# Gated cross-attention block: the last batch by halves of its queries, the last row tile's GELU and product in pieces, and new orders of all five engines

## What is computed

```
x = x + tanh(gx) * attention(layernorm(x), ctx, mask)     # 8 heads of 64, softmax, W_o, b_o
h = gelu(bitlinear(layernorm(x), w1, b1))                 # 512 -> 2048
x = x + tanh(gf) * bitlinear(h, w2, b2)                   # 2048 -> 512
bitlinear(x, w, b): x / rms(x), rounded to 8 bit by its row's largest |x|;
                    w rounded to -1, 0, 1 by its mean |w|; product, + b
```

## Time and profile before

| | |
|---|---|
| median of 3 runs | 1093.64 us (1092.78 to 1095.91) |
| the profiled execution: its time, its span | 1094.15 us, 1092.3 us |
| PE busy | 1025.8 us (94% of the span) |
| ACT, DVE, POOL busy | 856.0, 793.5, 768.4 us |
| mean granted TensorE clock | 0.979 |

### The profile page before, as it was taken

How to read it: one execution, slowest core, us unless ns; L and a number is a source line. 1 busy time by engine, 2 the same in 40 slices (tenths; PEclk the granted TensorE clock), 3 DMA queues, 4 the chain that set the end, 5 groups by cost and what they waited for, 6 DMA issues and landing times.

```text
span 1092.3 us, 23652 instructions
## 1 busy us (share of the span) xinstructions
PE 1025.8 (94%) x8372; PEld 614.6 (56%) x8372; DVE 793.5 (73%) x1620; ACT 856.0 (78%) x1445; POOL 768.4 (70%) x739
## 2 busy tenths in 40 slices
...
GB/s 302 210 219 156 181 138 191 137 151 148 156 167 122 173 169 133 165 141 188 118 188 126 144 178 139 182 119 187 141 144 150 140 184 136 159 122 155 151 63 81
DMA packets 480004, 170.76 MB, mean 156 GB/s; under 512 B 458256, under 2 KB 460048, under 8 KB 479504
## 3 DMA queue, kind: packets, MB, share of 16 engines
...
## 4 chain that ended last, share of the span: by engine, by line
PE 72%; POOL 10%; DMA 8%; ACT 4%; DVE 3%; issue 3%; SPq 1%; ACTq 0%; POOLq 0%; DVEq 0%
PE ps_g L548 36%; PE ps_s L578 10%; PE ps_g L645 9%; PE ps_g L601 8%; PE ps_g L637 8%; POOL p L991 5%; DMA pt<-p 4%; PE ps_g L589 2%; DMA hqt<-hq 2%; DMA xqt<-xq 1%; POOL p L986 1%; POOL ctx L1002 1%; ACT hq L937 1%; SPq L510 1%; DMA pt<-in_ctx 1%
## 5 line engine op out<-in xcount | busy, mean ns | idle before, releaser
L991 POOL TENSOR_TENSOR p<-prob,p 112x750 f16<-112x750 f32 x256 | 404.0, 1594 | 107.7 <-ACT p L879 106.2
L706 DVE CUSTOM_DVE_ANT_0 prob<-ps_s,mbias 112x750 f32<-112x750 f32 x256 | 232.1, 933 | 114.8 <-PE ps_s L578 114.1
L872 ACT ACTIVATE prob<-prob,rmin 112x750 f32<-112x750 f32 x256 | 233.4, 913 | 30.9 <-DVE rmin L706 30.5
L548 PE MATMUL ps_g<-ctx,wk 128*128 128x375 f16 x1152 | 198.8, 325 | 17.3 <-DVE wk L663 15.9
L548 PE MATMUL ps_g<-wv,ctx 128*128 128x512 f16 (+1 forms) x864 | 195.3, 380 | 1.2 <-DVE k_sb L728 0.9
L548 PEld LDWEIGHTS ps_g<-ctx,wk 128*128 128x128 f16 x1152 | 109.1, 98 | 95.6 <-issue 28.6
L578 PE MATMUL ps_s<-k_sb,q_sb 64*112 64x375 f16 x1536 | 149.2, 327 | 5.3 <-DVE rmin L706 5.3
L548 PEld LDWEIGHTS ps_g<-wv,ctx 128*128 128x128 f16 (+1 forms) x864 | 88.5, 103 | 96.5 <-DVE q_sb L733 1.9
L879 ACT ACTIVATE p<-prob 112x750 f16<-112x750 f32 x160 | 127.6, 817 | 16.1 <-DMA pt<-p 15.9
L601 PE MATMUL ps_g<-pt,v_sb 128*64 128x224 f16 x2304 | 123.8, 262 | 4.3 <-DMA pt<-p 3.7
L578 PEld LDWEIGHTS ps_s<-k_sb,q_sb 64*112 64x112 f16 x1536 | 89.4, 126 | 55.0 <-issue 34.9
...
## 6 DMA issues: line engine op xcount, KB each, us to landing
...
pt<-p SPq DMA_TRANSPOSE x256, 4.1
...
```

What stands on the lines that cost most here:

```text
L548: mm = nc.tensor.matmul(out, lhs, rhs, start=(m == 0), stop=(m == len(steps) - 1))
L706: nc.vector.tensor_tensor_reduce(prob[:, (b * NU + n) % PROBS, :].rearrange("p (c k) -> p c k", c=2), ps_s[0:HT, n % 2, :, 0:CH], mbias[:, ...
L872: nc.scalar.activation(prob[:, (b * NU + n) % PROBS, :], prob[:, (b * NU + n) % PROBS, :], ACT.Exp, bias=rmin[:, n:n + 1], scale=-1.0, acc ...
L991: nc.gpsimd.tensor_tensor(p16[:, u % HILO, 1, 0:J], prob[:, (b * NU + n) % PROBS, :], p16[:, u % HILO, 0, 0:J], ALU.subtract).then_inc(s[" ...
```

## The change

Three things are changed.

1. **The last batch goes by halves of its queries.** In batch 15 unit m is half m // 4 of pair m % 4: first all four pairs for queries 0 to 111, then all four for queries 112 to 223. There are eight products PV:0..7:15 of 112 columns in place of four of 224, eight PA, PL and R. O:0:15 (tile 26) needs PL of the first half alone, O:1:15 (tile 27) that of both. T:u:15 waits for its own place in `pt` unit by unit.
2. **The last tile in pieces.** For tile 27 the GELU (ZE), the squares (ZS), the maximum (ZM) and the rounding (Z3) go by quarters of 512 columns, ZA joins the quarters' maxima and sums, and the transposing (ZT) and F2:1:15 go in two halves.
3. **All orders are new.** `cycle` runs for b = 1..13 and no longer to 14; `end` holds the rest of batch 14 and batch 15, whose steps are mixed.

```diff
-FIRST, LAST = 1, 15
+FIRST, LAST = 1, 14
...
+        def pair_and_half(b, m):
+            return (m % NP, m // NP) if b == LB else (m // 2, half_of(b, m))
+        def queries_of(b):
+            return HT if b == LB else TQ
+        def attn_pieces(b, n):
+            size = queries_of(b)
+            at = (b * TQ + (n // NP * HT if b == LB else 0)) % RINGQ
+            first = min(size, RINGQ - at)
+            return [(0, at, first)] + ([(first, 0, size - first)] if first < size else [])
...
-                    need(sp, "weighted", 0, (b * NM + n // 2 - TURNED) // 2)
+                    if b == LB and n // 2 >= TURNED:
+                        need(sp, "weighted", b, n // 2 - TURNED)
+                    else:
+                        need(sp, "weighted", 0, (b * NM + n // 2 - TURNED) // 2)
...
+                elif kind == "ZT":
+                    sp.wait_ge(z_hq, NF // 2 * (n + 1))
+                    part = slice(n * F // 2, (n + 1) * F // 2)
+                    sp.dma_start_transpose(tail_hqt[:, n * KF // 2:(n + 1) * KF // 2, :], tail_hq[:, part])\
+                        .then_inc(d_zt[n], 16)
...
-                            mm = nc.tensor.matmul(g[e * DH:(e + 1) * DH, 0:TQ]
-                                                  .rearrange("p (a q) -> p a q", a=2),
-                                                  v_sb[:, p, t, va, (2 * n + e) * DH:(2 * n + e + 1) * DH],
+                            mm = nc.tensor.matmul(g[e * DH:(e + 1) * DH, 0:queries_of(b)]
+                                                  .rearrange("p (a q) -> p a q", a=len(units)),
+                                                  v_sb[:, p, t, va, (2 * j + e) * DH:(2 * j + e + 1) * DH],
...
-                    need(pe, "attn_lo", b, 2 * NP - 1)
+                    need(pe, "attn_lo", b, 2 * (NM if t == NR - 1 else NP) - 1)
...
+                        if t == NR - 1 and k % (KF // 2) == 0:
+                            pe.wait_ge(d_zt[k // (KF // 2)], 16)
...
+                elif kind == "ZM":
+                    dve.wait_ge(z_gelu, n + 1)
+                    nc.vector.tensor_reduce(maxs_z[:, n:n + 1], tail_h[:, n * 512:(n + 1) * 512], AX.X, ALU.max,
+                                            apply_absolute_value=True).then_inc(z_max, 1)
...
+                elif kind == "ZE":
+                    part = slice(n * 512, (n + 1) * 512)
+                    need_tile(act, "h_lin", NR - 1, n)
+                    nc.scalar.activation(tail_h[:, part], tail_h[:, part], ACT.Gelu).then_inc(z_gelu, 1)
+                elif kind == "ZS":
+                    part = slice(n * 512, (n + 1) * 512)
+                    act.wait_ge(z_gelu, n + 1)
+                    nc.scalar.activation(tail_hq[:, part], tail_h[:, part], ACT.Square, accum_out=sums_z[:, n:n + 1])\
+                        .then_inc(z_sq, 1)
```

More of the change, by code:

```diff
@@ L15 @@
 NB = 16
+LB = NB - 1
 TQ = 224
@@ L331, in build @@
         hi_act, hi_pool = sem("hi_act"), sem("hi_pool")
+        z_gelu, z_sq, z_max, z_hq = sem("z_gelu"), sem("z_sq"), sem("z_max"), sem("z_hq")
+        d_zt = [sem(f"d_zt{n}") for n in range(2)]
         d_res = [sem(f"d_res{n}") for n in range(HELD)]
@@ L566, in emit @@
                 if kind == "S":
-                    j, half = n // 2, half_of(b, n)
-                    if n % 2 == 0:
+                    j, half = pair_and_half(b, n)
+                    if n < NP if b == LB else n % 2 == 0:
                         need(pe, "q_lo", b, j)
@@ L585, in emit @@
                     need(pe, "recips", b, n)
-                    for m in range(2 * n, 2 * n + 2):
-                        at = 256 + half_of(b, m) * HT
+                    units = [n] if b == LB else [2 * n, 2 * n + 1]
+                    j = n % NP
+                    for m in units:
+                        at = 256 + (0 if b == LB else half_of(b, m) * HT)
                         for e in range(2):
@@ L591, in emit @@
                                              ident[0:HT, 0:HT], start=True, stop=True)
-                    for u in range(b * NU + 4 * n + 4 - HILO, b * NU + 4 * n + 4):
+                    for u in range(b * NU + 2 * units[0], b * NU + 2 * units[-1] + 2):
                         need_turned(pe, u)
@@ L595, in emit @@
                         need(pe, "v_lo", b, NT - 1)
-                    places = sorted((place_of(b, 2 * n), place_of(b, 2 * n + 1)))
-                    both = slice(places[0], places[1] + 1, places[1] - places[0])
+                    places = sorted(place_of(b, m) for m in units)
+                    both = slice(places[0], places[-1] + 1, max(1, places[-1] - places[0]))
                     steps = [(t, va, pa) for t in range(NT) for va, pa in ((0, 0), (1, 0), (0, 1))]
@@ L805, in emit @@
                                                    op0=ALU.mult, op1=ALU.add).then_inc(s["h_lin"], 1)
+                elif kind == "ZM":
+                    dve.wait_ge(z_gelu, n + 1)
+                    nc.vector.tensor_reduce(maxs_z[:, n:n + 1], tail_h[:, n * 512:(n + 1) * 512], AX.X, ALU.max,
+                                            apply_absolute_value=True).then_inc(z_max, 1)
+                elif kind == "ZA":
+                    c = (NR - 1) % 2
+                    dve.wait_ge(z_max, NF)
+                    nc.vector.tensor_reduce(smh[:, c, 2:3], maxs_z[:, :], AX.X, ALU.max).then_inc(s["h_max"], 1)
+                    dve.wait_ge(z_sq, NF)
+                    nc.vector.tensor_reduce(smh[:, c, 7:8], sums_z[:, :], AX.X, ALU.add).then_inc(s["h_sq"], 1)
                 elif kind == "GM":
@@ L883, in emit @@
                     need(act, "attn_raw", b, n - 1)
-                    nc.scalar.activation(rb[:, :], g[:, 256:256 + TQ], ACT.Copy).then_inc(s["recips_out"], 1)
+                    nc.scalar.activation(rb[:, 0:queries_of(b)], g[:, 256:256 + queries_of(b)], ACT.Copy).then_inc(s["recips_out"], 1)
                 elif kind == "PL":
```

170 lines of the change are left out of this document (97 added, 73 removed).

## The result

| | before | after |
|---|---|---|
| median of 7 runs each, us | 1095.91 (1092.78 to 1099.55) | 1089.88 (1084.89 to 1092.93) |
| ratio | 1 | 0.9938, 95% interval 0.991 to 0.9966 |
| profiled execution, its span, us | 1094.15, 1092.3 | 1088.55, 1086.8 |

The kernel is faster by 0.62% (6.0 us between the medians), where 1.3% was forecast; 1089.88 lies just inside the range. Five marks in PE's timeline divide the span. The first line is us from the start of the span, the others are distances in us.

A forecast was written before the change was run, and what follows sets the result against it. PE was taken as the bound from 120 to about 1010 us, its waits and a serial chain at start and end. Terms -1.5 - 1.5 - 1.6 - 2.67 - 6.9 = -14.2 gave span 1078.1, median 1079.5 us; range 1070 to 1091.

The forecast's parts named there:

- the start: The new start lists on all engines, before the steady cycles: -1.5 us, bounds -6 and +4.
- the difference of 3.1 and 1, less a little: In the start: S:4:0 and V:0:1 moved earlier (1.1 and 2 us), against about 1 us net for L:2 and L:3 later.
- the 10.4 us: PE's wait for a bank in the start of the kernel before, which moved steps were to fill in part.
- The wait near 52 us under 8: Sign in the new profile: PE's long wait in the start falls below 8 us.
- The cycle: The steady orders, 13 cycles: PE's waits for `hqt` go, -1.5 us, bounds -5.4 and +6.5.
- no new kind over 3 us: Sign in the new profile: from 125 to 940 us no new kind of PE wait exceeds 3 us.
- The rival of a stall in each cycle: ACT's L4 waits for DVE's L3, delaying PE's F1: 2.2 us per cycle, 13 times, +28.6, 1108 us; chance 0.10.
- The end up to the last PV: The end through the last product PV: PV:7 ends at 1044.8 against 1046.43 before, -1.6 us.
- rival one: Narrow PV products cost as much as wide ones: +4 us, 1083.5, or +10.8, 1090.3, at serial loads; chance 0.13.
- rival two: The two halves don't get ahead, POOL's wait at L:7:15 passing delays through: 1083.5 to 1087.5 us; chance 0.17.
- The last projection: Behind the last PV, one tile's output projection of 2.67 us where two took 5.34: -2.67 us.
- The tail: From the end of the last projection to the span's end: 31.5 us where before it took 38.4, -6.9.

The follow-up runs named there:

- e3: The changed kernel with GELU, squares, maximum, rounding and turning of tile 27 undivided; 1092.74 us, ratio 0.9963 to the kernel before.
- e4: The changed kernel with ACT's three context splits ahead of the two of x in the start, as before; 1086.95 us, ratio 0.9906.
- e9: The kernel of e4 with the scores of unit 3 (S:3:0) put back ahead of Q:3:0 on PE; 1087.44 us, ratio 0.9913.
- e8: The kernel of e1, with POOL waiting ahead of the low part of unit 1 until DVE has centred batch 2's queries; 1080.95 us, ratio 0.9854.
- e11: The kernel of e4, with POOL waiting ahead of WB:6:0 until DVE has rounded piece 4 (WQ:4:0); 1081.57 us, ratio 0.9861.
- e12: The kernel of e4 with POOL's start list of before, the other four engines' lists new; 1089.83 us, ratio 0.9934.
- e10: The kernel of e4 with the sums for the first mean (WA:2 to WA:7) ahead of E:1:0, H:0:0 and H:1:0 on ACT; 1087.64 us, ratio 0.9909.
- e14: The kernel of e11 with matmuls that nothing reads filling four idle stretches of PE in the end; 1080.69 us, ratio 0.9859.
- e15: The kernel of e14, with POOL waiting ahead of WB:4:0 as well, until DVE has rounded piece 2; 1079.96 us, ratio 0.9852.
- e2: The kernel before with only the new cycle lists; 1091.34 us, ratio 0.9944.
- e1: The changed kernel with the five start lists of before, on all engines; 1081.19 us, ratio 0.9847 to the kernel before.

## Why the prediction was wrong

The direction held and the size did not: the step that failed is **the start**. It stood in the sum with -1.5, bounds -6 and +4, "the difference of 3.1 and 1, less a little". Measured is +4.1, and +7.9 and +8.2 in e3 and e4. Point by point:

- **The start, the overlap.** The 3.1 us were S:4:0 and V:0:1, which were to "fill a part of the 10.4 us". They could not: PE runs its list in order, the step that waits is Q:0:1, and in both lists both steps stand behind it. They could fill only the 0.90 us that PE waited for `pt` ahead of PV:0:0. The new list even moves S:3:0 (1.17 us) from ahead of the wait to behind it, and S:4:0 then waited 2.00 for `rmin`. What moving S:3:0 back is worth isn't shown (e9). "The wait near 52 us under 8" failed: 10.06.
- **The start, the hold-up.** I put DVE's share at nothing, and never asked why it came so late to empty V:4. The row that answers it lay in the trace before: two centrings in 4.95 us beside POOL's work. The new order puts a W2 rounding in that place. Taking the centring's hold-up away gains nothing (e8), since PE then waits for the turned queries and the turned parts. For the rounding ACT waits, with V:5:0 and the next roundings behind it. In the profiles of e4 and e11 taking a part of this hold-up away is worth 2.9 us directly; 4.2 more lie at the clock behind it, which e9 and e12 show can differ without it. By the medians, e4, e9 and e10 have ratios of 0.9906 to 0.9913 and e11, e14 and e15, with POOL's wait, 0.9852 to 0.9861: some 5 of the 10 us that the new start costs. The rest stays open; the late first product (2.1 us) may be a part (e4).
- **The cycle.** -1.5 forecast, -1.9 in the kernel after, -3.6 in e2 and -4.0 in e1. The waits for `hqt` went, and those for `pt` nearly. But "no new kind over 3 us" failed: the low part brings 4.4, so by its waits the kernel after gains next to nothing here, and that -1.9 is so near to the forecast is in part luck. The rival of a stall in each cycle asked for 1.35 us in each. A wait does recur in 12 cycles, which I had named as a sign of being wrong, but of 0.4 us at most.
- **The end up to the last PV.** -1.6 forecast, -2.6 to -3.3 measured. A narrow head with spreading is 1.13 us, not 1.3, so rival one is refuted. Counted from the spreading of PV:3:13, HT of tile 24 was issued at 95.4 us (1032.20); 96.7 was forecast. POOL waited 2.28 us for tile 25's statistics and began L:7:15 at 1013.69. The halves do get ahead, which refutes rival two.
- **The last projection.** -2.67 forecast, -1.1 in the kernel after. The count was right; the size missed the clock, 4.67 us for what takes 2.75 at 1.0. The scaling ahead of it, which I had left at 2.1, fell to 1.67.
- **The tail.** 31.5 forecast; 30.75 (e1) and 30.86 (e4), with ACT's gap of 1.22 us that I had ruled out. In the kernel after it is 34.39, because F1 of tile 27 ran at the lower clock in that execution (6.42, forecast 3.6), and F2 took 0.8 more than in e1. I counted on one slow row. In fact any row of PE behind an idle gap may be slow: 6.42 behind 3.62 us, 4.67 behind 1.67, but 3.61 behind 3.34 (e1) and 2.75 behind 1.67 (e4). Which of them are differs between executions.

My sum without its start term was -12.7; e1, which is just that kernel, measured -15.8 in its profile. The duration of 1.59 us for L:1:0 is in POOL's second row, not in the last, and gave no term of its own.
